# Four chained attention layers on one core: narrow column tiles for the first layer's weighing, the last layer's first sum behind a weighing, and new order tables

## The reference

```python
# layer 0: 32 latent channels
th, ph, g = conv1x1(x, w_theta), conv1x1(x, w_phi), conv1x1(x, w_g)
x = gamma_sa * conv1x1(softmax(th.T @ ph) @ g.T, w_o) + x      # then a small attention over 128 concepts
# layer 1: queries and keys of 32 channels, values of 256
x = gamma * (v @ softmax(q.T @ k).T) + x
# layer 2: group norm (32 groups), one head of 256 channels, projection
x = x + proj(softmax(q @ k.T / 16) @ v)
# layer 3: group norm, 8 heads of 32 channels, projection, layer norm
x = layer_norm(softmax_per_head(q @ k.T * s) @ v @ wo.T + bo) + x
```

## Time and profile before

| | before |
|---|---|
| median of 3 runs | 2777.87 us (2777.54 to 2778.6) |
| profiled execution | 2775.3 us |
| its span | 2773.5 us |
| mean granted PE clock | 0.941 of 2.4 GHz |
| PE busy | 2573.6 us (93%) |
| DVE busy | 1887.9 us (68%) |
| ACT busy | 1286.2 us (46%) |
| POOL busy | 590.9 us (21%) |
| first stage | 0 to 396 us |
| six middle stages | 315.0, 324.1, 325.6, 324.8, 326.0, 324.1 us |
| last stage | 2335.6 to 2773.5 us |

### The profile page before, as it was taken

How to read it: one execution, slowest core, us unless ns; L and a number is a source line. 1 busy time by engine, 2 the same in 40 slices (tenths; PEclk the granted TensorE clock), 3 DMA queues, 4 the chain that set the end, 5 groups by cost and what they waited for, 6 DMA issues and landing times.

```text
span 2773.5 us, 26540 instructions
## 1 busy us (share of the span) xinstructions
PE 2573.6 (93%) x9892; PEld 1411.0 (51%) x9892; DVE 1887.9 (68%) x1925; ACT 1286.2 (46%) x2209; POOL 590.9 (21%) x322
## 2 busy tenths in 40 slices
PE   7989988999999999999999999999999999888887
PEld 4456654464645556364554646445563545543332
DVE  4544228686578866787586875777667875778885
ACT  3353222646345552645426463455626454144555
POOL 0082130050100401031010501104020320124473
PEclk8999997989999999999999899999999999989898
DMA  2000001010202002020200102020020201122200
GB/s 89 1 1 1 1 7 39 20 27 1 76 1 46 1 31 46 1 46 1 59 18 6 41 1 76 1 46 1 12 65 1 46 1 31 31 46 46 46 1 31
DMA packets 29297, 72.15 MB, mean 26 GB/s; under 512 B 10224, under 2 KB 10416, under 8 KB 28912
## 3 DMA queue, kind: packets, MB, share of 16 engines
q1 hardware_dynamic: 29168, 70.45, 10.2%
HBM read 11.40 MB, written 8.39 MB: 7 GB/s over the span
## 4 chain that ended last, share of the span: by engine, by line
PE 73%; DVE 17%; ACT 5%; issue 3%; POOL 1%; DMA 0%; DVEq 0%; SPq 0%; ACTq 0%; POOLq 0%
PE ps L633 11%; PE ps L666 10%; PE ps L652 9%; PE ps L784 8%; PE ps L954 7%; PE ps L875 6%; PE ps L641 6%; PE ps L788 4%; DVE ba_nmx L1335 3%; PE ps L722 2%; PE ps L861 2%; DVE fa_nmx L1335 2%; DVE accb L1503 2%; DVE bb_nmx L1335 1%; DVE tmp L1384 1%
## 5 line engine op out<-in xcount | busy, mean ns | idle before, releaser
L1188 ACT ACTIVATE prb<-ps 128x512 f32<-128x512 f32 x896 | 490.1, 602 | 316.0 <-PE ps L666 285.6
L1335 DVE TENSOR_REDUCE ba_nmx<-ps 128x1 f32<-128x1024 f32 x448 | 531.1, 1219 | 115.5 <-PE ps L652 113.7
L1503 DVE TENSOR_TENSOR accb<-accb,prb 128x1024 f32<-128x1024 f32 x312 | 392.9, 1288 | 107.1 <-ACT prb L1188 105.9
L666 PE MATMUL ps<-qs,ks 97*128 97x512 f32 x896 | 357.8, 474 | 30.9 <-DMA qs<-ba_nmx_r 16.0
L652 PE MATMUL ps<-ks,qs 96*128 96x512 f32 x896 | 335.0, 475 | 16.2 <-DVE ba_nmx L1335 14.9
L1049 ACT ACTIVATE pr<-ps 128x512 f32<-128x512 f32 x336 | 197.2, 601 | 315.9 <-PE ps L875 236.7
L555 POOL TENSOR_TENSOR q2k<-pr,q2k 128x512 fp32r<-128x512 f32 x112 | 143.7, 1299 | 812.4 <-ACT q2k L1086 812.4
L666 PEld LDWEIGHTS ps<-qs,ks 97*128 97x128 f32 x896 | 160.2, 197 | 277.8 <-ACT prb L1188 167.9
L954 PE MATMUL ps<-prb,vb 128*32 128x512 f32 x1792 | 251.1, 634 | 2.5 <-ACT prb L1188 2.5
L652 PEld LDWEIGHTS ps<-ks,qs 96*128 96x128 f32 x896 | 177.6, 208 | 122.8 <-DVE ba_nmx L1335 51.5
L545 POOL TENSOR_TENSOR acc<-pr 128x1024 f32<-128x1024 f32 x28 | 67.2, 2398 | 747.0 <-ACT pr L1049 626.6
(11 more groups left out here) (320 smaller groups left out, 3564.3 us busy)
## 6 DMA issues: line engine op xcount, KB each, us to landing
qs<-part SPq DMA_DIRECT2D x168, 128.0 KB, 2.5
ks<-part SPq DMA_DIRECT2D x168, 128.0 KB, 2.5
xm<-in_x SPq DMA_DIRECT2D x8, 1024.0 KB, 5.7
out<-prb SPq DMA_DIRECT2D x28, 256.0 KB, 2.2
q2k<-part SPq DMA_DIRECT2D x48, 128.0 KB, 2.4
w<-in_weights SPq DMA_DIRECT2D x1, 2592.0 KB, 8.7
out<-pr SPq DMA_DIRECT2D x4, 256.0 KB, 2.0
qs<-ba_nmx_r SPq DMA_DIRECT2D x56, 4.0 KB, 1.8
```

Of the source, the lines that this page charges most:

```text
L666: return pe.matmul(o.ps[:, bank, :], keys[0:ROW + 1, tile(jt)], queries[0:ROW + 1, cols(ic)], start=True, stop=True)
L1188: act.activation(weights3(o, s, g), o.ps[:, turn3[score_use(s, g) % 3], :], ACT.Exp)\
L1335: dve.tensor_reduce(o.nmx[:, head, it:it + 1], o.ps[:, bank:bank + 2, :], AX.XY, ALU.max, negate=True).then_inc(o.max_sb[n].sem, 1)
L1503: dve.tensor_tensor(o.sums[pair], o.pairs[(s - 1) % 2][pair] if j == 1 else o.sums[pair], o.pairs[s % 2][pair], ALU.add).then_inc(done.sem, 1)
```

## The change

Three things are changed.

1. Layer 0's `weigh` becomes four matmuls of 32 weight columns, at column tiles 0, 32, 64 and 96; what is computed is the same.
2. In layer 3's step NT+1 the first sum stands directly behind the weighing, in one slot with it, ahead of the second pair of scores; the turns of the banks follow.
3. All tables of `ORDER` are replaced (five engines in three parts).

```diff
     ("both", "PE"): (
-        0, 2, 2, 1, 1, 2, 1, 2, 4, 2, 3, 2, 4, 1, 5, 2, 2, 1, 1, 4, 1, 3, 3, 2, 1, 1, 2, 1, 1, 3, 2, 2, 1, 2,
+        0, 2, 2, 3, 1, 2, 1, 1, 3, 1, 1, 1, 3, 1, 4, 1, 2, 1, 3, 2, 1, 2, 2, 2, 3, 1, 1, 2, 2, 1, 1, 2, 1, 4,
...
         def score_use(s, g):
-            return QUAD * s + g + (s >= NT + 2)
+            return QUAD * s + g + ((s, g) >= (NT + 1, 2))
 
         def total_use(ic):
-            return (QUAD * (NT + 2), QUAD * STEPS3 + 1)[ic]
+            return (QUAD * (NT + 1) + 2, QUAD * STEPS3 + 1)[ic]
...
                         for j in range(2):
-                            mm = pe.matmul(o.ps[2 * L * j:2 * L * (j + 1), 2 + ic, :], o.vgo[:, 2 * jg + j, :],
-                                           o.pr[:, 2 * (s % 2) + j, :], start=jg == 0, stop=jg == 3,
-                                           tile_position=(0, 2 * L * j))
+                            for of in mixed:
+                                at = 2 * L * j + of.start
+                                mm = pe.matmul(o.ps[at:at + L, 2 + ic, :], o.vgo[:, 2 * jg + j, of],
+                                               o.pr[:, 2 * (s % 2) + j, :], start=jg == 0, stop=jg == 3,
+                                               tile_position=(0, at))
...
                             if s:
                                 weigh(s - 1)
+                                if s == NT + 1:
+                                    sum_weights(0)
                                 yield
                             yield from scores(s, 1)
-                            if s == NT + 1:
-                                sum_weights(0)
-                                yield
```

More of the change, by code:

```diff
@@ L77 @@
     ("fronts", "PE"): (
[20 rows of a table removed]
[19 rows of a table added]
     ("fronts", "ACT"): (
[3 rows of a table removed]
[3 rows of a table added]
     ("both", "ACT"): (
-        0, 3, 2, 1, 11, 1, 4, 2, 1, 2, 1, 1, 1, 2, 1, 1, 2, 2, 2, 1, 1, 2, 1, 2, 1, 3, 10, 1, 5, 1, 21, 1, 2,
-        2, 5, 2, 3, 39, 8, 2, 2, 1, 6, 1, 2, 1, 1, 1, 5, 1, 8, 1, 6, 1, 4, 1, 3, 1, 4, 1, 25, 1, 2, 1, 2, 2, 4,
-        3, 3, 1, 5, 15,),
+        0, 4, 13, 1, 1, 1, 1, 1, 1, 2, 4, 2, 3, 2, 1, 2, 1, 2, 1, 2, 2, 1, 1, 2, 1, 1, 8, 1, 5, 1, 21, 2, 2, 1,
+        5, 2, 3, 39, 12, 2, 1, 1, 4, 1, 7, 1, 6, 2, 8, 2, 5, 2, 5, 1, 24, 1, 5, 1, 3, 2, 1, 1, 5, 1, 1, 1, 3,
+        16,),
     ("backs", "ACT"): (
-        8, 74, 74, 47, 1, 1, 2, 1, 2, 2, 2, 1, 1, 1, 1, 2, 3, 3, 4, 2, 2, 1, 2, 2, 1, 1, 1, 1, 2, 1, 1, 1, 3,
-        3, 1, 1, 3, 1, 6, 2, 7, 1, 1, 1, 7, 1, 2, 1, 2, 1, 1, 1, 9, 1, 3, 1, 12,),
+        8, 74, 71, 2, 2, 1, 1, 56, 2, 2, 2, 1, 1, 1, 2, 1, 1, 1, 12, 1, 1, 1, 4, 2, 1, 1, 3, 1, 1, 1, 4, 1, 3,
+        1, 3, 1, 5, 1, 6, 2, 6, 1, 2, 1, 12, 1, 5, 1, 6,),
     ("fronts", "DVE"): (
-        2, 2, 2, 1, 1, 1, 7, 8, 5, 3, 3, 1, 1, 1, 4, 2, 1, 1, 2, 2, 1, 2, 5, 1, 1, 1, 1, 10, 24, 1, 1, 1, 3, 1,
-        10, 23, 1, 8, 1, 1, 1, 3, 2, 4, 5, 4, 50,),
+        3, 1, 1, 2, 1, 1, 7, 8, 5, 3, 3, 2, 6, 3, 1, 1, 2, 3, 6, 2, 1, 10, 27, 1, 1, 3, 10, 24, 1, 2, 1, 5, 2,
+        3, 1, 1, 1, 2, 1, 1, 3, 4, 50,),
     ("both", "DVE"): (
-        0, 2, 1, 1, 1, 2, 1, 1, 1, 6, 10, 3, 1, 2, 7, 3, 2, 2, 1, 1, 1, 1, 4, 2, 2, 1, 1, 9, 24, 1, 6, 1, 5,
-        15, 1, 4, 1, 1, 5, 2, 5, 1, 2, 2, 2, 1, 1, 1, 3, 1, 1, 1, 1, 1, 2, 1, 1, 1, 4, 2, 1, 2, 43, 1, 6, 1, 1,
-        1, 2, 1, 4, 2, 4, 2,),
+        0, 4, 1, 2, 1, 2, 2, 4, 11, 3, 1, 2, 3, 3, 2, 1, 3, 3, 6, 1, 1, 1, 1, 1, 1, 9, 26, 3, 9, 10, 1, 1, 1,
+        3, 1, 4, 2, 1, 3, 1, 6, 3, 1, 1, 2, 2, 1, 1, 2, 1, 2, 1, 3, 1, 1, 1, 3, 3, 1, 1, 46, 1, 2, 1, 1, 2, 7,
+        2, 4, 2,),
     ("backs", "DVE"): (
[3 rows of a table removed]
[3 rows of a table added]
     ("fronts", "POOL"): (
-        12, 2, 5, 3, 1, 1, 3, 1, 3, 17, 5, 2, 1, 1, 1, 1, 1, 4, 1,),
+        12, 1, 1, 1, 2, 1, 1, 1, 1, 1, 1, 1, 1, 1, 5, 17, 6, 1, 1, 3, 1, 3, 1, 1,),
     ("both", "POOL"): (
-        0, 14, 1, 18,),
+        0, 7, 1, 25,),
     ("backs", "POOL"): (
-        0, 9, 1, 5, 14, 10, 2, 1, 1, 2, 1, 1, 10,),
+        0, 9, 1, 5, 14, 11, 1, 1, 1, 1, 1, 1, 11,),
     ("fronts", "SP"): (
@@ L130 @@
     ("backs", "SP"): (
-        4, 4, 3, 1, 5, 2, 1,),
+        4, 4, 1, 1, 6, 2, 2,),
 }
```

## The result

The changed kernel takes 2738.3 us (median of four runs, 2736.66 to 2741.21) against 2777.7 of the kernel before: a ratio of 0.9861, 95% interval 0.9844 to 0.9878. The profiled execution has a span of 2736.9 us and a mean granted clock of 0.951 (2773.5 and 0.941 before).

A forecast was written before the change was run, and what follows sets the result against it. PE was taken as the bound (73% of the chain of waits, DVE 17%). Terms -7.0, -7.4 and -5.5 sum to -19.9 us on 2775.3, giving 2755.4; with 2.6 for the median, 2758 us, range 2744 to 2778.

The forecast's parts named there:

- part 3: End of layer 3's second maxima: PE's wait for the shift rows' DMA shrinks in six middle stages, -5.5 us.
- part 5: Remaining tables, first and last stage: 0, with 5 us either way in the last and 4 in the first.
- part 1: Tile modes on PE: fewer entries into narrow tiles and fewer unlike neighbours, weight loads hidden, -7.0 us.
- Part 2: Layer 3's group norm at stage heads: DVE's multiplication escapes POOL's add, PE's 1.24 us wait goes six times, -7.4 us.
- rival (d): Middle stages: one more half-clock stretch each, +30 against -20, 2788 us; chance 0.10, shared with a sum that waits.
- Part 4: Layer 3's first sum, right behind a weighing: its earlier wait for the adders costs 0, at most 7.4 us.
- (a): Only the tile-mode gain stays; the reordered norm and maxima bring their waits back elsewhere: 2771 us, chance 0.23.
- (b): No gain stays, as PE's saved time lies where ACT or DVE paces it: about 2778 us, chance 0.13.
- (c): Weight loads of the narrower weighing tiles are not hidden, +21 us: 2779 us in all, chance 0.02.

The follow-up runs named there:

- w64_new: The changed kernel with layer 0's weighing back in two tiles of 64 columns: 2746.30 us.
- shift_old: The changed kernel with PE's and DVE's order in layer 3's second maxima as before: 2754.84 us.
- fill_old: The kernel before with ten useless matmuls in PE's wait for the shift rows' DMA, in the six middle stages: 2770.85 us.
- tables_only: The kernel before with the new tables alone, layer 0's weighing in 64 columns and the first sum behind the second pair of scores: 2753.40 us.
- code_only: The kernel before with both code edits (32-column weighing, sum directly behind the weighing) and the old tables: 2806.16 us.
- gn_old: The changed kernel with PE's, ACT's and DVE's order from layer 3's group norm to the end of the first maxima as before: 2747.26 us.
- w32_old: The kernel before with layer 0's weighing in four tiles of 32 columns as its only edit: 2778.02 us.

## Why the prediction was wrong

The direction and the waits at the three places were right; the size was not, and the measured time lies under the range. Three steps failed: part 3 put the half-clock time behind the wait at nothing (16.5 us measured for 5.5), part 5 put the last stage's tables at nothing with 5 us to either side (12.6 measured), and part 1 counted PE time alone (15 us measured for 7). By its own steps:

- **Part 1 (modes), -7.0.** The prices held: a second weighing adds 0.85 us, an unlike neighbour 0.15 (most pairs of unlike weighings in `w64_new` take 2.00 to 2.01 us, the like pairs of the changed kernel 1.85), and loads are hidden. The step's 1.20 - 0.85 is 0.35, not 0.33, which is half a microsecond over the run. What failed is the value, taken as PE time times the chain's share. Undone one at a time in the changed kernel, columns and sum cost 8 and 12 us. Half-clock time moves with them, 35 and 14 us in the traces (29 and 21 by the medians of all executions), and with the sum 3.2 us of waits; the step had no term for either.
- **Part 2 (group norm), -7.4.** Right: undone, it costs 9.0 us, with the forecast's own rows back in place. One sentence of it was loose: PE does not do fewer score groups by the projection, one stands ahead of the norm now; ACT's order is what keeps POOL's add off L1419. And its lower end, another add on another scale, did come true elsewhere: in the first stage, with 2.45 us of PE's time.
- **Part 3 (shift rows), -5.5.** The waits were sized about right, by another path, and what stands behind them was left out. The step counted DVE's work ahead of the cast; the rows show that the shift rows come no earlier, and that PE has one weighing more to do meanwhile. The wait fell by 10.9 us, of which, by `shift_old`, 4.7 came back as other waits. But undone, the piece costs 16.5 us, with 58 us more of half-clock time. The rows were there: the earlier trace rows shows 0.51 right behind the wait, and the forecast used them for rival (d) alone, as a loss that might come, and not as a loss that would go.
- **Part 4 (the merged sum), 0.** The value held only because the new tables put front work behind it, as the part said for the middle stages. The bound did not hold: it counted the wait of the sum and not that of the next user of its bank. Under the old tables the 14 waits for ACT's logarithm cost 19.9 us.
- **Part 5 (the other tables), 0, with 5 and 4 us to either side.** The last stage's tables brought 12.6 us and the first's lost 8.7. Both lie outside what was allowed; a stage in which PE waits 62 us has more to give than 5. Where in the last stage's first half the gain arises stays open.
- **The clock.** Over the run half-clock time falls by 62 us; by 0.1 to 0.2 us each that is 6 to 12 of the 39 us, an estimate. Rival (d) priced it at 0.5; the kernel loses less, since other engines set part of the pace there, as PE's longer wait for DVE in `fill_old` shows.

The single pieces sum to more than the whole: 8 + 12 + 9 + 16.5 + 12.6 - 8.7 = 49 us against 39. Each was undone with all else new, and an order made for one code edit is worse without it, as `tables_only` and `code_only` show from both sides: 24 us gained, 29 lost, 39 gained together.

Of the rivals, (a) and (b) are out by `gn_old` and `shift_old`, (c) by `w32_old` and `w64_new`; of (d), the clock did count, with the opposite sign.

## What to carry to other kernels

When a wait goes, read the granted clock of the stretch behind it and add what the half-clock time there costs; here the piece was worth three times the forecast of its wait. When a step is moved ahead of others that share its buffers in turn, follow the next user of its buffer too, not only what the step itself waits for. And when order tables are replaced, test them stage by stage: one of three was a loss, in part from a collision that had been taken out elsewhere, and putting it back made the best kernel of this study, 2729.6 us.

## What the runs showed of the hardware that was not expected

Ten matmuls of no use, in a PE wait of 2.7 us, raised the granted clock of the next 10 us from 0.51 to 0.87 and took 6.5 us off the run. A microsecond at 1.2 GHz cost this kernel 0.1 to 0.2 us (estimates from three readings: 0.08, 0.16 and 0.2), not 0.5. The collision of DVE's 128x2 multiplication with POOL's add came back to the hundredth of a microsecond (2.04 us against 0.16) when the order was put back: DVE's ends 0.02 us behind POOL's, 1365.73 and 1365.71.
